# A second sequence's scores in one piece, masked expansions computed transposed, the gate's bias on VectorE, and a convolution tap folded into a matmul

## The reference, cut to what matters

```python
# embedding correction, dom in -1..7, W_exp (8, 32, 256), W_proj (8, 256, 32)
base = emb_table[token_ids]; dom = domain_map[token_ids]; out = base
for d in range(8):
    expanded = einsum('bsd,ed->bse', base, W_exp[d])
    out = out + 0.1 * einsum('bse,de->bsd', expanded, W_proj[d]) * (dom == d)
# attention: softmax over 128 keys for each of 16 heads (scores, exponentials, weighted sum)
# gate: softmax(x @ gate_w + gate_b), weights under 0.1 dropped, the rest rescaled to sum 1
# recurrence inputs, x normalised, xp its copy padded with 3 zero steps
conv_out  = sum(xp[:, j:j+T, :] * conv_w[:, j] for j in range(4))
projected = (x + conv_out) @ in_w.T + in_b
delta     = tanh(x @ dt_w.T + dt_b) @ tr_w.T
```

## Time and profile before

| | us |
|---|---|
| median of 3 runs | 633.06 |
| lowest and highest | 633.02, 637.52 |
| the profiled execution | 638.58 |
| its span, first to last instruction | 636.6 |
| around the span | 1.98 |

### The profile page before, as it was taken

How to read it: one execution, slowest core, us unless ns; L and a number is a source line. 1 busy time by engine, 2 the same in 40 slices (tenths; PEclk the granted TensorE clock), 3 DMA queues, 4 the chain that set the end, 5 groups by cost and what they waited for, 6 DMA issues and landing times.

```text
span 636.6 us, 9352 instructions
## 1 busy us (share of the span) xinstructions
PE 540.7 (85%) x3047; PEld 328.1 (52%) x3062; DVE 464.3 (73%) x1219; ACT 246.7 (39%) x769; POOL 177.9 (28%) x300
## 2 busy tenths in 40 slices
PE   2788969999999998998998998984669898989884
PEld 2665446555555555555555654631335555555553
DVE  1354657778778778778778777485689999999852
ACT  1363036236336336326326326613334444343321
POOL 6406560131132222213213213021232424233110
PEclk9888969999999999999999998995679999999997
DMA  6701100000000000000000000004200000000000
GB/s 183 252 2 35 34 17 1 2 0 0 0 0 0 0 0 0 0 0 0 0 0 0 0 0 2 1 3 83 48 0 9 18 9 18 9 18 12 14 16 16
DMA packets 13517, 12.75 MB, mean 20 GB/s; under 512 B 2795, under 2 KB 12724, under 8 KB 13492
## 3 DMA queue, kind: packets, MB, share of 16 engines
q1 hardware_dynamic: 12212, 10.34, 6.2%
q0 software_dynamic: 1280, 2.11, 1.2%
HBM read 8.25 MB, written 2.10 MB: 16 GB/s over the span
## 4 chain that ended last, share of the span: by engine, by line
PE 36%; DVE 27%; issue 12%; POOL 10%; ACT 7%; SPq 3%; DMA 2%; another core or an unknown queue 1%; DVEq 0%; POOLq 0%
PE psum L634 13%; ACT probs L976 4%; SPq L380 3%; POOL rstd L424 3%; PE psum L574 3%; POOL hq L494 3%; DVE stats L1260 2%; PE psum L552 2%; DVE neg_max L1283 2%; POOL rstd L421 2%; PE psum L727 2%; PE psum L696 2%; DVE hsc L1207 2%; PE psum L709 2%; DVE n_tok L1272 2%
## 5 line engine op out<-in xcount | busy, mean ns | idle before, releaser
L634 PE MATMUL psum<-expw_sb,n2T 128*128 128x512 f32 x256 | 119.1, 609 | 0.0
L421 POOL TENSOR_TENSOR rstd<-meanvar,ln_eps_col 128x1 f32<-128x1 f32 x64 | 20.9, 326 | 286.3 <-DVE meanvar L1264 286.1
L896 PE MATMUL psum<-wguT,n2T 128*128 128x512 f32 (+1 forms) x192 | 82.6, 582 | 0.0
L976 ACT ACTIVATE probs<-psum,neg_max 128x128 f32<-128x128 f32 x256 | 69.1, 391 | 33.1 <-DVE neg_max L1283 32.9
L634 PEld LDWEIGHTS psum<-expw_sb,n2T 128*128 128x128 f32 x256 | 47.2, 195 | 47.6 <-issue 47.6
L918 PE MATMUL psum<-wdT,probsT 128*128 128x256 f32 x192 | 50.1, 404 | 16.1 <-ACT probsT L944 16.1
L1120 ACT ACTIVATE probs<-u_now 64x16 f32<-64x16 f32 x128 | 27.6, 215 | 83.3 <-DVE u_now L1524 81.1
L896 PEld LDWEIGHTS psum<-wguT,n2T 128*128 128x128 f32 x192 | 38.0, 199 | 39.3 <-issue 34.2
L1283 DVE TENSOR_REDUCE neg_max<-psum 128x4 f32<-128x512 f32 x64 | 40.4, 681 | 19.1 <-PE psum L578 10.3
L494 POOL TENSOR_TENSOR hq<-wgu_tmp,hsc 128x704 f32<-128x704 f32 x16 | 22.5, 1404 | 109.2 <-DVE wgu_tmp L1222 109.2
L918 PEld LDWEIGHTS psum<-wdT,probsT 128*128 128x128 f32 x192 | 35.0, 195 | 29.2 <-issue 23.9
(11 more groups left out here) (167 smaller groups left out, 992.2 us busy)
## 6 DMA issues: line engine op xcount, KB each, us to landing
expw_sb<-in_expert_w SPq DMA_DIRECT2D x8, 256.0 KB
expw_sb<-hidden SPq DMA_DIRECT2D x16, 128.0 KB
result<-res SPq DMA_DIRECT2D x16, 128.0 KB
w_raw<-in_w_down SPq DMA_DIRECT2D x1, 704.0 KB
w_raw<-in_w_gate SPq DMA_DIRECT2D x1, 640.0 KB
w_raw<-in_w_up SPq DMA_DIRECT2D x1, 640.0 KB
wexp_sb<-in_w_expand SPq DMA_DIRECT2D x1, 256.0 KB
wproj_sb<-in_w_project SPq DMA_DIRECT2D x1, 256.0 KB
```

Of the source, the lines that this page charges most:

```text
L634: last = mm(pq[:, g, :], n2T[:, u, k, :], expw_sb[:, k, EPQ * g:EPQ * (g + 1), :].rearrange("p e n -> p (e n)"), start=(k == 0), stop=(k = ...
L896: last = mm(pgu[u][:, c0:c1], xqT[:, u, k, :], wguT[:, k, c0:c1], start=(k == 0), stop=(k == KD - 1))
L976: last = nc.scalar.activation(probs[:, u, h, :], pq[:, g, j * T:(j + 1) * T], ACT.Exp, bias=neg_max[:, u, h:h + 1])
```

## The change

1. **Scores.** TensorE issues `expand(0)`, `expand(1)` and the recurrence inputs, then `scores(1, ...)` for all four banks in one piece, so it waits for all four `p_ready[g]` at once. Behind them come `project(0)`, `delta`, the first transposes of probabilities, `project(1)`, and the rest; the transposes of bank 3 are behind `attend(0, 1)`. ScalarE's tanh moves behind all exponentials of sequence 0.
2. **Expansion transposed.** `expand(c)` makes 128 rows of the expansion for both sequences (`wexp` as the weights, `xT` streamed). The mask is then one comparison and multiplication (`is_equal`, `mult`) with a column of domain numbers `dom_of`; the token's domain comes along as a third 128-column chunk of `x_tok`, filled by GpSimd and transposed by TensorE. The transposes and copies of `e_tok` go, and so do the routing steps of VectorE.
3. **Gate bias** by VectorE: one addition on 128x8 (`g_sum`) in front of the maximum; the two-record matmul goes, and the bias is loaded to all 128 partitions.
4. **Last tap.** The input itself and its last tap are multiplied by `ownw_sb` = in_w * (1 + conv_w[3]), computed once, with the rank's 16 columns in the same matmul (80 columns). The convolutions have one tap less (VectorE 3 steps for 4, GpSimd 5 for 7).
5. **VectorE's order.** `weights(1)` to `weights(4)` come behind the correction's additions and statistics, ahead of `ln_apply(0, ...)`.

```diff
-POOL_STEPS = 2 * TAPS - 1
+DVE_STEPS = TAPS - 1
+POOL_STEPS = 2 * TAPS - 3
@@ gpsimd @@
-                        pool.tensor_copy(x_tok[:, u, :], seq(hidden, i + 1, u)).then_inc(base_copied, 1)
+                        pool.tensor_copy(x_tok[:, u, D:], own_domain(i + 1, u).to_broadcast([T, 128])).then_inc(base_copied, 1)
+                        pool.tensor_copy(x_tok[:, u, 0:D], seq(hidden, i + 1, u)).then_inc(base_copied, 1)
@@ tensor: gate, recurrence inputs, expansion @@
-                    mm(pback[u][:, 0:EXPERTS], ones_row[:], gateb_sb[:], start=True, stop=False)
+                def own_inputs(u0, u1, behind):
...
+                        last = mm(pback[0][0:STATE + RANK, u0 * T:u1 * T], ownw_sb[:, k, :],
+                                  n3T[:, u0:u1, k, TAPS - 1:], start=(k == 0), stop=False, skip_group_check=True)
+                def earlier_inputs(u0, u1, steps, counts):
...
+                        last = mm(pback[0][0:STATE, u0 * T:u1 * T], inw_sb[:, k, :],
+                                  mixed[:, k, u0:u1, :].rearrange("p u t -> p (u t)"),
+                                  start=False, stop=(k == KD - 1), skip_group_check=True)
-                        last = mm(pfront[u][:, 0:D], xT[:, u, k, :], wexp_sb[:, k, :],
+                        last = mm(pfront[c][:, 0:2 * T], wexp_sb[:, k, c * 128:(c + 1) * 128], xT[:, :, k, :],
-                        transposes(pfront[u], x_tok[:, u, :]).then_inc(baseT_done, 1)
+                        transposes(pfront[u], x_tok[:, u, :], chunks=KD + 1).then_inc(baseT_done, 1)
@@ tensor: order @@
                 if front:
                     expand(0)
+                    expand(1)
                 if rec:
                     recurrence_inputs()
...
-                if back:
-                    scores(1, (0, 1))
-                if front:
-                    expand(1)
...
-                    scores(1, (2, 3))
...
+                if back:
+                    scores(1, range(QUARTERS))
...
+                if front:
+                    project(0)
+                if rec:
+                    delta(0, 2, 1, pback[1])
@@ scalar @@
-                        if g == 3 and rec:
-                            rank_inputs(0, 2, 1)
                         exps(0, g)
+                    if rec:
+                        rank_inputs(0, 2, 1)
-                if front:
-                    masked_transposed(0)
-                    masked_transposed(1)
@@ vector @@
+                    V.tensor_tensor(g_sum[:, u, :], pback[u][:, 0:EXPERTS], gateb_sb[:], ALU.add).then_inc(gate_sum, 1)
-                    for j in (TAPS - 1, *range(TAPS - 1)):
+                    for j in range(TAPS - 1):
+                    V.scalar_tensor_tensor(out=eT[:, c, :, :], in0=xT[:, :, KD, :], scalar=dom_of[:, c:c + 1],
+                                           in1=pfront[c][:, 0:2 * T].rearrange("p (u t) -> p u t", u=2),
+                                           op0=ALU.is_equal, op1=ALU.mult).then_inc(masked, 1)
...
-                    weights(1)
-                    weights(2)
-                    weights(3)
-                    weights(4)
                 if front:
                     for u in (0, 1):
                         dve.wait_ge(proj_done, fn[u])
...
+                if back:
+                    for k in range(1, 5):
+                        weights(k)
```

More of the change, by code:

```diff
@@ L138, in tower @@
         woT_sb = early[:, 5 * D:7 * D].rearrange("p (k n) -> p k n", k=KD)
[L140 to L143 removed]
+        x_tok = sb("x_tok", [T, 2, D + 128])
+        xT = sb("xT", [128, 2, KD + 1, T])
+        eT = sb("eT", [128, KD, 2, T])
         n_tok = sb("n_tok", [T, 2, D])
@@ L407, in _ @@
             pool.memset(ln_eps_col[:], LN_EPS).then_inc(pool_set, 1)
-            for d in range(DOMAINS):
-                pool.memset(dom_no[:, d:d + 1], float(d)).then_inc(pool_set, 1)
             pool.wait_ge(pool_set, CONSTANTS)
@@ L559, in body @@
                 fbefore, fn = counts(pe, i + 1) if front else (None, None)
+                copied = [4 * (i + 1) + 2 * u + 2 if isinstance(i, int) else pe.snap(4 * i + (2 * u + 6)) for u in (0, 1)]
                 def scores(u, quarters):
@@ L663, in project_in @@
-                def project_in(u, steps, counts):
-                    pe.wait_ge(p_stored, sequences(pe, i, u))
+                def own_inputs(u0, u1, behind):
+                    pe.wait_ge(n3T_ready, sequences(pe, i, u1 - 2 * behind))
+                    if not behind:
+                        pe.wait_ge(dt_ready, sequences(pe, i, u0))
+                        pe.wait_ge(p_stored, sequences(pe, i, u0))
+                    for k in range(KD):
+                        last = mm(pback[0][0:STATE + RANK, u0 * T:u1 * T], ownw_sb[:, k, :],
+                                  n3T[:, u0:u1, k, TAPS - 1:], start=(k == 0), stop=False, skip_group_check=True)
+                    last.then_inc(rank_done, u1 - u0)
@@ L711, in compress, with expand @@
                     last.then_inc(lat_done, 1)
-                def expand(u):
-                    pe.wait_ge(xT_ready, fn[u])
+                def expand(c):
+                    pe.wait_ge(xT_ready, fn[1])
                     for k in range(KD):
-                        last = mm(pfront[u][:, 0:D], xT[:, u, k, :], wexp_sb[:, k, :],
+                        last = mm(pfront[c][:, 0:2 * T], wexp_sb[:, k, c * 128:(c + 1) * 128], xT[:, :, k, :],
                                   start=(k == 0), stop=(k == KD - 1))
                     last.then_inc(expand_done, 1)
-                def masked_transposed(u):
-                    pe.wait_ge(masked, fn[u])
-                    transposes(pfront[u], e_tok[:, u, :]).then_inc(maskT_done, 1)
                 def project(u):
-                    pe.wait_ge(eT_ready, fn[u])
-                    for k in range(KD):
-                        last = mm(pfront[u][:, 0:D], eT[:, u, k, :], wproj_sb[:, k, :],
-                                  start=(k == 0), stop=(k == KD - 1))
+                    pe.wait_ge(masked, fn[1])
+                    for c in range(KD):
+                        last = mm(pfront[u][:, 0:D], eT[:, c, u, :], wproj_sb[:, c, :],
+                                  start=(c == 0), stop=(c == KD - 1))
                     last.then_inc(proj_done, 1)
@@ L1223, in fp4 @@
                                            op1=ALU.subtract).then_inc(steps[7], 1)
+            for d in range(DOMAINS):
+                k, p = divmod(d * EXPAND, 128)
+                V.memset(dom_of[p:p + EXPAND, k:k + 1], float(d)).then_inc(domains_set, 1)
             V.memset(v_aug[:], 1.0).then_inc(dve_set, 1)
@@ L1456, in body @@
                     weights(0)
-                    maxima(1, (0, 1))
-                if front:
-                    expanded(1)
-                if back:
-                    maxima(1, (2, 3))
+                    maxima(1, range(QUARTERS))
                     if rec:
```

174 lines of the change are left out of this document (63 added, 111 removed).

## The result

The changed kernel takes 639.18 us in the median of 20 runs (636.94 to 642.79); the kernel before takes 633.04 us beside it (20 runs, 632.18 to 640.29). The ratio is 1.0069, 95% interval 1.0046 to 1.0092. That is outside the forecast range of 625.5 to 638.0, and on the other side of no change.

A forecast was written before the change was run, and what follows sets the result against it. VectorE's and ScalarE's chain was taken as the bound, not TensorE. Terms of -3.75 us plus 2.2 for clock falls gave -1.55 on the profiled 638.58; carried to the 633.06 median, 631.5 us, range 625.5 to 638.0.

The forecast's parts named there:

- A steady pair: -0.43: Net change of one steady loop pair at unchanged clock, -0.43 us, bounds -1.3 and +0.4; counted six times, -2.6 us.
- TensorE idle 1.9 us: Ahead of sequence 1's scores in a steady pair: TensorE stands idle 1.9 us, where it stood 0.48.
- +0.45: VectorE's third copy in a steady pair ends 0.45 us later through one-piece scores, the shorter convolution already included.
- I carry the difference over to it: From profile to median: the 5.5 us between profiled execution and median carried over, 633.06 - 1.55 = 631.5 us.
- one piece spares one such stop: Pair 0: one-piece scores avoid one TensorE stop like the 1.60 us one; -0.3 us, bounds -1.5 and +1.0.
- 2 of five steady pairs x 1.1: Clock falls behind the scores' wait in two of five steady pairs, about 1.1 us each: +2.2 us.
- Pair 7 I count as a steady one, -0.45: The last pair: taken to gain like a steady pair, -0.45 us.
- the chain is bare: Behind the loop: shorter last convolutions and the merged rank matmul count openly, -0.8 us.
- Rival 1: Clock stays up in all pairs: -3.75 us, 629.3 us; chance 0.23.
- Rival 2: TensorE is the bound and its removed work counts in full: 621.8 us; chance 0.13.
- rival 3: Slower: clock falls behind the scores' wait in every pair and again in the experts, 642 us; chance 0.12.
- Rival 4: Pair's end: GpSimd's doubled copies hold back VectorE's n_tok, +2.1 us in seven pairs, 633.6 us; chance 0.10.

The follow-up runs named there:

- b_tap: Kernel before with only the last tap put in the rank's columns, three convolution steps for four: 630.47 us, ratio 0.9919.
- b_gate: Kernel before with only the gate's bias added by VectorE instead of by a TensorE matmul: 633.38 us, ratio 0.9986.
- a_fill: Changed kernel, one piece kept, with VectorE's weights step 4 moved behind attention_out of sequence 0: 634.55 us, ratio 0.9963.
- b_onepiece: Kernel before with only the order change: both expansions first, sequence 1's scores in one piece, tanh behind sequence 0's exponentials: 650.16 us, ratio 1.0236.
- a_split: Changed kernel with sequence 1's scores issued in two pieces, banks 0 and 1, then 2 and 3: 629.01 us, ratio 0.9909.
- b_again: Kernel before, unedited, run again for a second profile: 635.61 us, ratio 1.0008; its profiled execution 632.27 us.
- a_comp: Changed kernel, one piece kept, with sequence 1's compression moved into the wait ahead of the gate: 639.20 us, ratio 1.0046.
- a_w4: Changed kernel, one piece kept, with the last pair's fourth weights job moved behind sequence 0's last probabilities and their transposes: 636.93 us, ratio 1.0012.
- a_warm: Changed kernel with four extra matmuls, result unused, in the wait ahead of sequence 1's scores: 635.46 us, ratio 0.9984.
- a_split_w4: Changed kernel with sequence 1's scores in two pieces and the last pair's fourth weights job behind sequence 0's last probabilities: 625.33 us, ratio 0.9843.
- a_split_w4_fill: Changed kernel with two-piece scores, last pair's fourth weights job later, and VectorE's weights step 4 behind attention_out of sequence 0: 626.54 us, ratio 0.9824.

## Why the prediction was wrong

**Right.** The bound: VectorE's and ScalarE's chain, not TensorE. "A steady pair: -0.43" was -0.38 at the full clock (48.38 for 48.76); `attention_out` came 19.13 us behind the convolution for 19.04 by my steps. "TensorE idle 1.9 us" was 2.00. *Convolution* -0.75 was -0.73 (b_tap). *Gate* +0.08 was +0.13 (b_gate), with the added addition at 0.17 us (0.13 the second time) for 0.20. The copy of the domains takes 0.29 us for 0.25 and is hidden. Falls in "two of the five steady pairs" came out as two; that was a guess, and a_fill with the same wait had one, b_onepiece with 2.3 us five. And the -0.43 is partly luck: in it stand one piece at +1.2 (the "+0.45" has the convolution's -0.75 in it) and VectorE's order with the early projections at -0.95. By differences of the runs they were +0.75 (against a_split) and about -0.53 (a_split against b_tap and b_gate), so two terms, each too large, cancelled.

**The carry.** "I carry the difference over to it" is the largest single step, 5.5 of the 7.7 us. On the profiled execution's own terms I forecast -1.55, and the two profiled ones differ by +0.6. But the one before stands 5.5 us above its own median, with the clock down at 24 and 37.75 us, and the one after is at its median. The step took it that the changed kernel wouldn't keep those falls; its profiled execution has them, at 24 and 38 us. I had seen that execution's distance to the median and asked only how large it was, not which stretches of the trace made it. The small +0.6 is luck too: in pair 0, where I had -0.3, the two differ by -2.2, in pair 1 by -0.6 where I had 0.0, and this hides +2.1 in pairs 2 to 6 (I had 0.05) and +1.2 behind the loop (I had -1.25).

Against b_again's profiled execution, which is at the lower end of its kernel's runs, the changed kernel's is 6.9 us longer: start +1.5, pair 0 +1.3, pair 1 +0.05, pairs 2 to 6 +2.2, behind the last `v_aug` +1.8. The first two aren't shown to come from the change: up to the first `v_aug` the sixteen traces take 28.5 to 32.4 us whatever the kernel, and pair 0 takes 49.7 to 53.4 with the old order and 49.9 to 51.8 in the five kernels with the changed one in one piece. What can be laid to the change are the last two, 4.0 us; the lowest runs of the two kernels differ by 4.8. My reason for pair 0, "one piece spares one such stop", was wrong: TensorE waits 2.98 us there for 1.60, and with two pieces (a_split) the pair takes 47.21 for 51.08.

**The clock, price per pair.** "2 of five steady pairs x 1.1" was 2 x 2.0. The first fall costs 1.5, since the projections and the transposes behind the scores run at the lower level too, and a second comes in the experts. Its condition stood in my third rival, "the later idleness ahead of the gate (0.7 and 1.3 us by the above) brings it down again", with 1.0 for it; in the forecast itself I left it out, although both rest on the same wait. a_comp shows that this wait decides whether a pair that fell falls again.

**Pair 7 and behind the loop.** "Pair 7 I count as a steady one, -0.45" and "-0.8" came out as +1.2 against the same execution, +1.8 against b_again. Half of the +1.8 lies ahead of the last `hidden`, the last sum of the experts. The last pair's order isn't a steady one's: of TensorE's jobs with the weights I didn't ask which copy of ScalarE each waits for. a_w4 shows 2.1 us at `attention_out`.

The other half lies behind it, because "the chain is bare" was wrong. The last `hidden` starts two paths. One goes through the last convolution to the last `drive`, and the change makes it shorter: 9.2 us in b_again, 8.0 in b_tap, 7.3 in the changed kernel. The other is sixteen transfers of `hidden`, issued one behind the other, on average 1.4 us apart, by SyncE (L380); VectorE's third addition beside the recurrence (L1492, L1530 before) waits for the last of them. From the end of `hidden` to that addition all sixteen traces take 26.5 to 27.2 us. b_again, then the changed kernel:

```profile
448.73 0.42 DVE L1530 TENSOR_TENSOR expw_sb<-psum,expw_sb 128x256 f32<-128x256 f32 x1 [0.82 <-DMA expw_sb<-hidden]
```

```profile
455.22 0.42 DVE L1492 TENSOR_TENSOR expw_sb<-psum,expw_sb 128x256 f32<-128x256 f32 x1 [3.29 <-DMA expw_sb<-hidden]
```

What the shorter path won, 2.0 us, this wait took back, and 0.5 us more, as the transfers themselves ended that much later. That is why the time from the last `drive` to the end grows, 201.9 us for 199.0, though the change doesn't touch anything there. Of the nine other kernels that are built on the changed one, four have 199.6 to 200.1 us there and five 201.2 to 202.2; in the four this wait is 1.8 to 2.0 us long, in the five 2.7 to 3.1. The wait stood in the trace that I predicted from, with 1.53 us. b_tap has it at 1.85, so the tap's gain behind the loop is what lies ahead of `hidden`, and the clock. No run moved the transfers; this is read from the traces. Where the remaining 0.4 us behind the last `hidden` come from stays open.

**The other rivals.** Rival 1 (the clock stays) did not happen; where the clock was nearly kept (a_warm) the time is 0.9984 of before and not 629 us, since pair 7 and the tail stay long. Rival 2 is out by b_gate. The first half of rival 3, a fall behind the scores in every pair, is what b_onepiece shows; its second, the fall in the experts, came there in no pair (the gate's wait is 0.51 to 0.54 us). In the changed kernel both came, in two pairs. Rival 4 is not borne out. VectorE's `n_tok` at the pair's end beside GpSimd's doubled copies, first VectorE, then GpSimd:

```profile
183.89 0.41 DVE L1237 TENSOR_SCALAR n_tok<-hidden,meanvar,rstd 128x256 f32 x1 [0.93 <-POOL rstd L422]
```

```profile
183.81 0.29 POOL L452 CAST x_tok<-dom_i 128x128 f32 x1
184.04 0.52 POOL L453 COPY x_tok<-hidden 128x256 f32 x1
184.51 0.29 POOL L452 CAST x_tok<-dom_i 128x128 f32 x1
184.75 0.40 POOL L453 COPY x_tok<-hidden 128x256 f32 x1
```

`n_tok` takes 0.41 us, as it does with no copy beside it, though GpSimd's cast had begun 0.08 us ahead of it. It is GpSimd's 128x256 copy, begun 0.15 us behind `n_tok`, that takes 0.52 instead of 0.40. By the rule of the Trainium skill, "SBUF — State Buffer", section "SBUF: two separate sides", whichever of the two starts first gets the shared ports for its whole instruction, where VectorE's is of the kinds that the section names. No trace shows whether `n_tok` is one. I had weighed only the half of it in which VectorE waits, and that half doesn't show in these rows; the engine that begins later is the one that loses, but 0.12 us and not the 0.26 for which they overlap.

**In sum,** by the runs: the tap -0.8%, the gate nothing; the early projections with VectorE's order about -0.5 us a pair, which is a difference between kernels and wasn't run by itself, as the transposed masks weren't. The one piece gives back 1.6% (0.75 us a steady pair on the chain, 3.9 us in pair 0, the rest clock) and the misplaced job of the last pair 0.6 to 0.7% (a_w4 and a_split_w4 by their ratios).

## What to carry to other kernels

When work is merged or taken off an engine that isn't the bound, list the waits that grow on TensorE and price each one's fall of the clock, not only the first; splitting the wait (1.6% here) was worth more than the matmuls saved (the gate's, nothing). Before a difference is carried from one profiled execution to a median, find the stretches that make this execution differ from the median. The last pass through a loop that has another order needs its own walk along the queues. And before a gain at the end is counted in full, ask what else starts from the same result: here the transfers of `hidden` ran beside the chain, and took longer.

## What the runs showed of the hardware

The length of a wait alone doesn't tell whether the clock falls. Behind 2.0 us it fell in two of five like pairs (the changed kernel, a_w4, a_comp) or in one (a_fill), behind 2.26 to 2.31 in five of five (b_onepiece), behind 1.48 to 1.49 in one of five (a_split_w4) or none (a_split), behind 1.50 to 1.51 in five of five (a_split_w4_fill); behind 0.51 to 0.59 never, in the steady pairs of the kernel before and of a_comp. All these are counts in one profiled execution each. A gain of 0.6 us on VectorE shifted the loop so that a fall that came in one pair (a_split_w4) came in all five (a_split_w4_fill), and the whole gain was gone; why the one and not the other falls stays open.
